# A hybrid block on one Trainium2 core: the feed-forward tail written out per engine, and half of the next norm made elsewhere and later

## The reference

```
x = x + attention_a(layernorm(x))   # 16 query heads over 4 key heads, softmax
x = x + ffn(layernorm(x))
x = x + attention_b(layernorm(x))   # linear attention, causal, no softmax
x = x + ffn(layernorm(x))           # the same weights again

def ffn(x):
    gf = global_net(mean over the tokens of x)          # one number for each batch
    out = x
    for _ in range(3):                                  # "cycles" 0, 1, 2
        tf = sigmoid(gelu(gelu(gelu(out @ w1 + b1) @ w2 + b2) @ w3 + b3) @ w4 + b4)
        coupling = 0.1 + ar * (0.7 * gf + 0.3 * tf - 0.5) * 2
        out = out + coupling * twist(out)               # twist: quarters of the features swapped, two negated
    return out
```

## Time and profile before

| what | us |
|---|---|
| median of 3 runs | 2151.23 (2150.05 to 2151.80) |
| the profiled execution | 2154.36 |
| its span, first to last instruction | 2152.4 |
| stretch 1604.5 to 1687.4: tail of the first feed-forward, and the start of the linear attention | 82.9 |
| stretch 1687.4 to 1950: linear attention | 262.6 |
| stretch 2092.9 to 2149: tail of the second feed-forward | 56.1 |

### The profile page before, as it was taken

How to read it: one execution, slowest core, us unless ns; L and a number is a source line. 1 busy time by engine, 2 the same in 40 slices (tenths; PEclk the granted TensorE clock), 3 DMA queues, 4 the chain that set the end, 5 groups by cost and what they waited for, 6 DMA issues and landing times.

```text
span 2152.4 us, 47834 instructions
## 1 busy us (share of the span) xinstructions
PE 2008.2 (93%) x13990; PEld 821.5 (38%) x13990; DVE 1814.5 (84%) x3396; ACT 1496.7 (70%) x2955; POOL 159.8 (7%) x290
## 2 busy tenths in 40 slices
PE   6699999999999999999999999989985899998984
PEld 4323333333333333333333333344432566665431
DVE  6789999999999999999999999934557677776456
ACT  4438888888888888888888888844558544446656
POOL 1340000000000000000000000010004101002001
PEclk9769999999999999999999999999997999999996
DMA  6421121121122122122122122131000000000002
GB/s 165 136 67 43 44 72 52 44 71 53 43 71 53 43 71 54 42 71 55 42 69 56 42 70 56 34 126 46 1 1 1 1 0 1 1 0 1 1 1 79
DMA packets 110229, 101.30 MB, mean 47 GB/s; under 512 B 52240, under 2 KB 91424, under 8 KB 110096
## 3 DMA queue, kind: packets, MB, share of 16 engines
q1 hardware_dynamic: 110096, 99.92, 17.2%
HBM read 78.79 MB, written 20.77 MB: 46 GB/s over the span
## 4 chain that ended last, share of the span: by engine, by line
PE 82%; DVE 6%; ACT 4%; issue 3%; SPq 3%; DMA 1%; ACTq 0%; POOL 0%; DVEq 0%; POOLq 0%
PE ps L697 22%; PE ps L672 15%; PE ps L720 10%; PE ps L726 10%; PE ps L840 6%; PE ps L847 3%; PE ps L900 3%; PE ps L909 2%; PE ps L929 2%; PE ps L948 2%; ACT YT L1088 1%; PE ps L686 1%; PE ps L979 1%; SPq L423 1%; DVE mx L1395 1%
## 5 line engine op out<-in xcount | busy, mean ns | idle before, releaser
L1395 DVE TENSOR_REDUCE mx<-ps 128x1 f32<-128x512 f32 x2048 | 1279.7, 683 | 20.2 <-PE ps L672 15.4
L1088 ACT ACTIVATE YT<-ps 128x512 f32<-128x512 f32 x2048 | 1058.1, 606 | 253.4 <-PE ps L726 253.3
L697 PE MATMUL ps<-YT,work 128*32 128x512 f32 x4096 | 546.1, 605 | 0.0
L672 PE MATMUL ps<-work 64*128 64x512 bf16 x2048 | 460.8, 389 | 17.7 <-DVE mx L1395 14.2
L720 PE MATMUL ps<-work 64*128 64x512 bf16 x2048 | 401.7, 378 | 1.7
L726 PE MATMUL ps<-work 34*128 34x512 bf16 x2048 | 398.3, 378 | 0.0
L672 PEld LDWEIGHTS ps<-work 64*128 64x128 bf16 x2048 | 144.6, 93 | 622.0 <-DVE mx L1395 548.3
L720 PEld LDWEIGHTS ps<-work 64*128 64x128 bf16 x2048 | 162.1, 94 | 106.0 <-ACT YT L1088 31.7
L847 PE MATMUL ps<-work,c_s 128*128 128x512 f32 x192 | 101.5, 655 | 30.9 <-ACT work L1139 30.9
L697 PEld LDWEIGHTS ps<-YT,work 128*32 128x32 f32 x4096 | 80.7, 108 | 122.8 <-issue 86.9
L726 PEld LDWEIGHTS ps<-work 34*128 34x128 bf16 x2048 | 101.0, 94 | 49.0 <-issue 1.3
(11 more groups left out here) (176 smaller groups left out, 1781.2 us busy)
## 6 DMA issues: line engine op xcount, KB each, us to landing
work<-k_scr SPq DMA_DIRECT2D x640, 64.0 KB, 2.1
work<-q_scr SPq DMA_DIRECT2D x640, 32.0 KB, 1.8
o_scr<-o_sb SPq DMA_DIRECT2D x32, 256.0 KB, 2.2
X<-in_L_attn_a_x_dram SPq DMA_DIRECT2D x8, 512.0 KB, 7.4
work<-negt SPq DMA_DIRECT2D x256, 1.0 KB
work<-o_scr SPq DMA_DIRECT2D x16, 256.0 KB
work<-inv_scr SPq DMA_DIRECT2D x16, 256.0 KB
out_dram<-X SPq DMA_DIRECT2D x8, 512.0 KB, 2.9
```

Source lines behind the costliest of these rows:

```text
L672: mm(ps[:, bank_of[x], :], qa[rows, p, jp, qt * P:(qt + 1) * P], ka[rows, p, kc_ * CH:(kc_ + 1) * CH], start=True, stop=True).then_inc(a_m ...
L697: m = mm(ps[32 * j:32 * j + 32, 7, :], vst[:, p, t, :], prob(GROUP * t + j), start=t == 0, stop=t == KTILES - 1)
L1088: fn(prob(u), ps[:, S_BANK + u % S_RING, :], ACT.Exp, scale=HD ** -0.5).then_inc(exp_ok, 1)
L1395: dve.tensor_reduce(mx[:, p, at_:at_ + 1], ps[:, bank_of[x], :], AX_X, ALU.max).then_inc(a_max, 1)
```

## The change

On each engine the loop over n now ends with item 16 (17 on PE), and what is left is written out, one call after the other, with an order of its own for each engine. `LAST` is 17. The calls of a pair follow one another more closely, and a result is asked for by the next engine sooner behind the instruction that makes it. The items, their layers and their instructions are the same; this holds for both feed-forwards.

For k = 0 two more things change. The `spread` of chunks 0 to 3 goes from ACT to POOL, where it is two tensor_tensor instructions of 128x1024 (times the root, plus the shift, each row broadcast) in place of four of ACT. And the norm, transposes and copies of chunks 4 to 7 (`TAIL` is 4) leave the feed-forward: `moments_of`, `root`, `spread` (on ACT), `turn_chunk` and `put_rows` of these chunks stand in tiles 0 to 4 of the linear attention, whose first tiles are written out to hold them. The linear attention thus starts when chunks 0 to 3 are in YT.

```diff
+LAST = (CYCLES - 1) * NCH + 1
+TAIL = BATCH * CPG // 2
...
 def turn_bank(st, c, kt):
+            if st == 2 and c >= TAIL:
+                return 5 + kt
...
 # PE, feed_forward
-                for n in range(SLOTS + R_LAG):
+                for n in range(LAST + 1):
...
+                fourth(LAST - 3)
+                second(LAST)
+                second(LAST + 1)
+                third(LAST - 1)
+                second(LAST + 2)
+                fourth(LAST - 1)
+                third(LAST + 1)
+                second(LAST + 3)
+                fourth(LAST + 1)
+                second(LAST + 4)
+                third(LAST + 3)
+                if k == 0:
+                    pe.wait_ge(f_d, NCH)
+                    pe.wait_ge(f_ga, 6)
+                    turn_chunk(2, 0)
+                second(LAST + 5)
+                fourth(LAST + 3)
+                second(LAST + 6)
+                if k == 0:
+                    project_qk(0, 0)
+                third(LAST + 5)
+                if k == 0:
+                    turn_chunk(2, 1)
+                fourth(LAST + 5)
+                if k == 0:
+                    project_qk(1, 1)
+                    turn_chunk(2, 2)
+                    turn(0, 0)
+                    turn_chunk(2, 3)
+                    pe.wait_ge(n_y, 2 * (2 * NCH + TAIL))
+                    project_vg(0, 0)
 # PE, linear attention, pipeline(n)
+                if isinstance(n, int) and 1 <= n <= TAIL:
+                    turn_chunk(2, TAIL + n - 1)
                 if is_tile(n - 2):
                     out_proj(n - 2, p)
                 if is_tile(n - 1):
                     norm_turn(n - 1, 1 - p)
+                if isinstance(n, int) and 1 <= n <= TAIL:
+                    pe.wait_ge(n_y, 2 * (2 * NCH + TAIL + n))
 # ACT, feed_forward (the first third of what is written out)
+                coupled(LAST + 1)
+                coupled(LAST + 2)
+                second(LAST - 1)
+                third(LAST - 3)
+                first(LAST)
+                fourth(LAST - 3)
+                first(LAST + 1)
+                second(LAST)
+                coupled(LAST + 3)
+                first(LAST + 2)
+                coupled(LAST + 4)
+                second(LAST + 1)
+                third(LAST - 1)
+                first(LAST + 3)
+                turned_rows(0)
+                fourth(LAST - 1)
...
 # ACT, linear attention, pipeline(n)
+                if isinstance(n, int) and 1 <= n <= TAIL:
+                    put_rows(2, TAIL + n - 1)
...
+                if isinstance(n, int) and n < TAIL:
+                    spread(2, TAIL + n)
 # DVE, feed_forward
+                update(LAST)
+                update(LAST + 1)
+                update(LAST + 2)
+                update(LAST + 3)
+                last_coupling(0)
+                update(LAST + 4)
+                joined(0)
+                if k == 0:
+                    moments_of(2, 0)
+                update(LAST + 5)
+                joined(1)
+                last_coupling(1)
+                update(LAST + 6)
+                if k == 0:
+                    moments_of(2, 1)
+                joined(2)
+                last_coupling(2)
+                if k == 0:
+                    moments_of(2, 2)
+                joined(3)
+                if k == 0:
+                    moments_of(2, 3)
+                joined(4)
+                last_coupling(3)
+                if k == 0:
+                    clear_tiles()
+                    rope_products(0, 0, 0)
+                    rope_sums(0, 0)
+                joined(5)
+                if k == 0:
+                    rope_products(1, 1, 1)
+                    rope_sums(1, 1)
+                joined(6)
+                joined(7)
 # DVE, linear attention
+            moments_of(2, TAIL)                    # ahead of tile 0
+                if isinstance(n, int) and n + 1 < TAIL:
+                    moments_of(2, TAIL + n + 1)    # at the end of pipeline(n)
 # POOL
+            def spread(c):
+                g = 2 * NCH + c
+                by = [norm4[:, c, i].rearrange("p (t n) -> p t n", n=1).broadcast_to((P, 4, DIM)) for i in range(2)]
+                pool.wait_ge(n_sh, g - NCH + 1)
+                pool.wait_ge(n_t, 2 * (g - 1))
+                pool.tensor_tensor(xn[:, c % 2], X[:, tiles(c), :], by[0], ALU.mult).then_inc(n_sp, 1)
+                pool.wait_ge(n_sp, c + 1)
+                pool.tensor_tensor(xn[:, c % 2], xn[:, c % 2], by[1], ALU.add).then_inc(n_xn, 1)
```

More of the change, by code:

```diff
@@ L819, in global_net @@
                     m.then_inc(f_g, 1)
[L821 to L845, removed]
-                        for kt in range(KT):
[L847 to L852, removed]
-                        for o in range(2):
[L854 to L867, removed]
@@ new lines, in second, with third @@
+                def second(n):
+                    pe.wait_ge(f_a1, base + n + 1)
+                    wait(pe, f_a2, base + n)
+                    for kt in range(KT):
+                        m = mm(ps[:, 2, :], c2_s[:, kt, :], h1[:, n % 2, kt, :], start=kt == 0, stop=kt == KT - 1)
+                    m.then_inc(f_h2, 1)
+                def third(n):
+                    pe.wait_ge(f_a2, base + n + 2)
+                    wait(pe, f_th, k * 2 * NCH + firsts(n))
+                    wait(pe, f_ze, (k * NCH + ended(n)) // 2)
+                    for o in range(2):
+                        m = mm(ps[64 * o:64 * o + 64, 3, :], c3_s[:], h2[:, (n + o) % 4, :], start=True, stop=True)
+                    m.then_inc(f_h3, 1)
@@ new lines, in first @@
+                def first(n):
+                    y, c = ORDER[n]
+                    if y == 0:
+                        act.wait_ge(f_h1, k * 2 * NCH + firsts(n + 1))
+                    else:
+                        act.wait_ge(f_up, k * 2 * NCH + updates(n + 1))
+                    wait(act, f_h2, base + n - 1)
+                    for mt in range(KT):
+                        m = fn(h1[:, n % 2, mt, :], ps[:, mt, :] if y == 0 else summed(c)[:, mt, :], ACT.Gelu,
+                               bias=bias[:, D1 + mt:D1 + mt + 1])
+                    m.then_inc(f_a1, 1)
+                    if y == 0:
+                        act.copy(summed(c), ps[:, 0:KT, :]).then_inc(f_as, 1)
@@ new lines, in second, with third @@
+                def second(n):
+                    act.wait_ge(f_h2, base + n + 1)
+                    wait(act, f_h3, pairs + n // 2 - 1)
+                    fn(h2[:, n % 4, :], ps[:, 2, :], ACT.Gelu, bias=bias[:, D2:D2 + 1]).then_inc(f_a2, 1)
+                def third(n):
+                    act.wait_ge(f_h3, pairs + n // 2 + 1)
+                    wait(act, f_z, pairs + n // 2 - 1)
+                    fn(h3[:, n // 2 % 2, :], ps[:, 3, :], ACT.Gelu, bias=bias[:, D3:D3 + 1]).then_inc(f_a3, 1)
@@ L1185, in feed_forward @@
                         spread(st, n + 2)
-                    layers(n)
+                    first(n)
+                    if n >= 1:
+                        second(n - 1)
+                    if n % 2 == 1 and n >= 3:
+                        third(n - 3)
+                    if n % 2 == 0 and n >= 4:
+                        fourth(n - 4)
                     if n % 2 == 1 and is_update(n + 1):
```

207 lines of the change are left out of this document (116 added, 91 removed).

## The result

The changed kernel takes 2130.0 us (median of 4 runs, 2124.9 to 2132.4) where the kernel before takes 2151.5 on the same chip (2150.1 to 2154.2): a ratio of 0.9893, 95% interval 0.9877 to 0.9909. In a second series it was 2130.5 against 2152.3, ratio 0.9894 (0.9878 to 0.9909). The forecast was 2132.0.

The account below looks back on a forecast made before the run. It took DVE to end both tails, no engine being full there, and PE to bound the linear attention. Second tail 12, first tail 11.8, tiles -5 made 19 us: 2151.2 - 19 = 2132, range 2118 to 2142.

Parts of the forecast that it names:

- Second tail: End of the second feed-forward: the new order alone gives back DVE's waits, a gain of 12 us.
- The three waits: DVE's second-tail waits for ACT's `z_end` (6.5), `coupled` (5.3) and `turned_rows` (3.8): 12.7 of 15.6 us go.
- First tail: End of the first feed-forward: DVE's load bounds it; `attend` of tile 0 comes 11.8 us earlier.
- the price of POOL's spread: First tail: DVE loses nearly all the time POOL streams, 16.6 of 18.7 us.
- 4.5 us longer groups: First tail: `joined` groups (L1602, L1607) of chunks 1, 3 and 4 some 4.5 us longer.
- PE's order there: First tail: PE waits for POOL's first spread, item 22's layer two 3 us late for ACT; counted as nothing.
- Tiles: Linear attention: four moved chunks add transposes and waits on PE, costing 5 us, bounds 4.4 and 9.
- Signs named ahead: Expected in profile: L1896 and L1898 2.3 to 2.7 us, tile 0 energy 12 to 14 earlier, second-tail DVE waits under 4.
- two signs of being wrong: L1607 keeping 1.43 us beside POOL's spread, or DVE's waits in the second tail staying above 8 us.
- No contention (2121): First tail rival: POOL and DVE share or hardly meet, so 2121 us, down to 2118; chance 0.28.
- stay ACT's (2142): Rival: both tails stay bound by ACT and half clock; second gives 6, first 3 net of tiles; chance 0.12.
- starve (2155): First tail rival: DVE's back-to-back instructions stretch POOL's eight to twice 2.34 us, giving 2155 us; chance 0.06.

Follow-up runs that it names:

- e1: The kernel before with the new written-out order for the second feed-forward only; 2143.0 us, ratio 0.9963.
- e3: The changed kernel with the spreads of chunks 0 to 3 on ACT again; 2118.7 us, ratio 0.9851, and 2121.5 us when repeated.
- e4: The changed kernel with POOL's two spread instructions a chunk replaced by four memsets of the same size, scaling left out; 2125.9 us, a single time.
- f3: The kernel before with only the spread of chunks 0 to 3 moved to POOL, all else in the old order; 2159.0 us, ratio 1.0035.
- f1: e3 with the moments of chunks 5 to 7 set behind the gated product and variance in the linear attention's tiles; 2119.6 us.

## Why the prediction was right, and where its sizes were off

- **Second tail, forecast 12.** 11.1 measured in the profile, 8.9 in the medians of e1. The three waits went as said, and 4.8 us remained where I had counted 2.9. Those of `joined(2)` and `joined(3)` came as added up (1.29 and 0.85 for 1.1 and 0.9). The one that I missed is `joined(0)`'s, 2.08 us in place of 0.7: a layer two and a layer three below full clock stood ahead of the turned rows. PE, second tail after:

```profile
2086.71 2.54 PE L849 MATMUL ps<-work,c_s 128*128 128x512 f32 x4 [2.10 <-ACT work L1177]
2089.18 1.98 PE L858 MATMUL ps<-work,c_s 128*64 128x512 f32 x4
```

  L858 takes 1.08 us at the full clock (2096.85), and ACT waited 1.23 us for it with `turned_rows(0)` queued behind. In the first tail of the same profile the two calls took 1.95 and 1.08, and `joined(0)` waited 0.58. The forecast had taken 0.7 off its 12.7 for layers at half speed; 1.5 of them stood here (0.6 + 0.9). The clock did not stay as low as I had said: 0.82 in place of 0.74.
- **First tail, forecast 11.8 up to `attend` of tile 0.** `attend` is 18.0 us nearer to update 17. The frame held: DVE's load bounds the tail, 61.9 busy of 64.1, and `attend` (L986) waited for DVE's masks (L1688):

```profile
1674.39 2.45 DVE L1688 TENSOR_TENSOR work<-ps,causal 128x512 f32<-128x512 f32 x4
1676.90 1.08 PE L986 MATMUL ps<-work 128*32 128x128 f32 x32 [0.20 <-DVE work L1688]
```

  The mis-sized term is the price of POOL's spread, 16.6 put down and 11.6 measured: the instructions took 1.92 to 2.07 and not the 2.34 of the bias addition (18.7 less 15.8, or 2.9), and 4.2 us of them, not 2, cost DVE nothing. The other 1.2 of the 6.2 us between forecast and measurement are DVE's idle time up to the masks (2.4 in place of 3) and its load without the price (53.9 in place of 54.4). That DVE stops for nearly as long as POOL streams, read from the one copy of the earlier trace rows, was right, and it caught `last_coupling`'s small instructions too, which I had left out. Of the 4.5 us longer groups forecast for chunks 1, 3 and 4, chunk 1 came nearest (3.4); the other two were 1.7 longer, and the rest of the cost went to L1587 and L1591.
- **PE's order there.** PE did not wait for the first spread, though I had said that it would: the spread ended at 1630.6, and PE was in a layer three at half clock until 1632.2. The transposes then ended at 1634.1, later than my 1632, and ACT was busy meanwhile. It cost nothing that the rows show, as counted.
- **Tiles, forecast 5, bounds 4.4 and 9.** 7.1 (and 6.7 in the second series). The transposes took 1.04 where I took 1.09 from the earlier trace rows; the wait ahead of energy was 0.5 in tile 1 and none in the others; and tile 1 paid 3.2, 1.76 of it for moments set ahead of the gated product. I had said that DVE hides them at about 1 us a tile in its 61 free ones: a free share over 262 us says nothing of the 2 us in which PE waits.
- **Sum.** Forecast 19 us; medians 21.5. The gain of the first tail was undersized by 6, the cost of the tiles by 2, and the gain of the second tail oversized by 1. The last two cancel half of the first, so the 2130 is nearer to the 2132 than the terms deserve: that part is luck.
- **Signs named ahead.** Missed: L1896 and L1898 at 2.3 to 2.7 us (1.9 to 2.1), energy of tile 0 earlier by 12 to 14 us (18.7, counted from update 17), and DVE's waits in the second tail under 4 (4.8). Neither of the two signs of being wrong appeared.
- **Rivals.** No contention (2121) is refuted by the 4.84 and 3.13 of L1607. I had priced contention at 11 us. No run has exactly that rival's case: in e3, 9 to 11 us faster, ACT carries the spreads, and in e4 POOL's writes still cost DVE something. The first tail itself gave back 5.6 and 7.3 us in e3 and its repeat, and 7.2 in e4. The tails do not stay ACT's (2142): DVE waits 4.8 us in the second and is busy 61.9 of 64.1 in the first. POOL does not starve (2155): its mean is 1.98 us, DVE is the one that waits. But a part of that rival's outcome can be had: f3 shows that POOL's spread alone, in the old order, makes the kernel slower, 2159.

## What to carry to other kernels

When an engine is idle, ask what its instructions read before giving it work: POOL's streams over SBUF were free of charge on POOL and cost the bounding DVE three quarters of their length. A tail that waits on a serial chain of small steps can be shortened by moving the chain's last links into a stage with a full engine: here 20 us out (up to 6 of them perhaps a matter of order) and 6 in, the largest single gain of those tried. Put the added step behind the instruction for which the full engine waits, not just somewhere in a stage with free share.

## What the runs showed of the hardware that I had not expected

- A DVE instruction of 0.17 to 0.28 us on 8 to 16 columns is stopped for up to the rest of POOL's 2 us instruction (1.74, 1.87), so small instructions lose by far the most in proportion.
- `TENSOR_SCALAR` on 256 columns is stopped by POOL's memsets (four take 1.35 alone, 1.98 and 2.49 beside them), `TENSOR_TENSOR` with two SBUF inputs is not (1.43).
- POOL's `TENSOR_TENSOR` on 128x1024 takes 1.89 to 2.07 us with a second input that repeats one value over 256 columns, 2.34 with a bias row that repeats over the four tiles. I didn't test what makes the difference.
- The stretch between the tiles and the second tail, with the same instructions in it, took 358.5 to 365.8 us in the profiles here. In the shortest (e3) the granted clock over 1950 to 2000 was 1.00, in the changed kernel 0.92; but f1 had 1.00 there too and took 361.5. What decides it was not tried.
